# Second normalisation moved from the gate phase into the second attention pass

## The reference

```
x = x + conv1x1(gn(x), weight[unique(labels)]) + bias           # L0
x = x + linear_attention(gn(x))                                 # L1: qkv and a 5x5 depthwise + pointwise copy of it, 32 heads of 16, projection, batch norm
x = x + spatial_gate(gn(x))                                     # L2
x = x + softmax_attention(gn(x))                                # L3: v = gn(x); out = gamma * o + v
gn(v) = (v - mean) / sqrt(var + 1e-5), over a group of 8 channels and 49 positions
```

## Time and profile before

| | |
|---|---|
| median of 3 runs | 2304.32 us (2300.87 to 2311.59) |
| the profiled execution | 2306.92 us, its span 2305.0 us |
| TensorE busy | 1888.4 us (82%) |
| VectorE busy | 1408.7 us (61%) |
| ScalarE busy | 898.2 us (39%) |
| GpSimd busy | 274.6 us (12%) |
| moved by DMA | 279.45 MB |

### The profile page before, as it was taken

The page is one execution under the profiler, slowest core; times in us unless marked ns, Lnnn a source line. Parts: engine busy times, 40 slices in busy tenths (PEclk is TensorE's granted clock), DMA queues, the critical chain, the costliest instruction groups (busy, mean ns, idle before and its releaser), DMA issues. The chain is left out here.

```text
span 2305.0 us, 40585 instructions
## 1 busy us (share of the span) xinstructions
PE 1888.4 (82%) x15572; PEld 1215.3 (53%) x15572; DVE 1408.7 (61%) x2847; ACT 898.2 (39%) x2181; POOL 274.6 (12%) x77
## 2 busy tenths in 40 slices
PE   2799999999999999778778999994377776876768
PEld 1355555566666665566656677762134443444446
DVE  4676677765555554322222455554899989999984
ACT  0444444444444445333333444441123333233332
POOL 1000000000000000000000000001243434434340
PEclk9899999999999999899888999997578888887879
DMA  2122322375657656888878665642112112121101
GB/s 96 46 81 71 105 71 77 113 197 171 188 166 215 187 163 165 191 222 217 214 220 218 164 153 160 156 113 74 42 42 70 46 54 70 57 68 56 59 28 43
DMA packets 264469, 279.45 MB, mean 121 GB/s; under 512 B 208788, under 2 KB 234772, under 8 KB 264280
## 3 DMA queue, kind: packets, MB, share of 16 engines
q1 hardware_dynamic: 264120, 276.59, 42.8%
q0 software_dynamic: 160, 0.26, 0.0%
HBM read 161.21 MB, written 115.61 MB: 120 GB/s over the span
## 5 line engine op out<-in xcount | busy, mean ns | idle before, releaser
L484 DVE TENSOR_TENSOR vk<-p_vk,mask_vo 128x512 f32<-128x512 f32 x256 | 176.8, 691 | 556.7 <-PE p_vk L378 556.7
L1449 POOL TENSOR_TENSOR rstd<-var,minus_half 128x32 f32<-128x32 f32 x32 | 173.9, 5433 | 1896.3 <-DVE var L1025 1896.3
L414 PE MATMUL p_dw<-tw,qd 98*64 98x98 f32 x3072 | 244.0, 295 | 90.7 <-ACT agg_out L627 63.2
L414 PEld LDWEIGHTS p_dw<-tw,qd 98*64 98x64 f32 x3072 | 200.4, 206 | 154.7 <-ACT agg_out L627 80.7
L627 ACT ACTIVATE agg_out<-p_dw 128x294 f32<-128x294 f32 x256 | 106.4, 416 | 332.2 <-PE p_dw L414 254.0
L600 ACT ACTIVATE half_b<-p_qkv 98x384 f32<-98x384 f32 x256 | 125.2, 489 | 233.6 <-PE p_qkv L337 231.7
L437 PE MATMUL p_g<-o,w_proj 128*128 128x392 f32 x512 | 206.5, 529 | 3.0 <-DVE var L540 2.4
L337 PE MATMUL p_qkv<-w_qkv,half_a 128*98 128x384 f32 x512 | 190.8, 496 | 6.7 <-DVE half_a L556 6.7
L337 PE MATMUL p_qkv<-w_qkv,z_odd 128*98 128x384 f32 x512 | 190.4, 495 | 1.8 <-DVE z_odd L556 1.8
L390 PE MATMUL p_out<-vk,qr 128*49 128x136 f32 x2048 | 173.6, 291 | 1.0 <-DVE oN L499 1.0
L635 ACT ACTIVATE o<-p_turn 128x196 f32<-128x196 f32 x256 | 85.2, 333 | 163.0 <-PE p_turn L399 162.1
(11 more groups left out here) (176 smaller groups left out, 3191.4 us busy)
## 6 DMA issues: line engine op xcount, KB each, us to landing
qkv_scratch<-half_b SPq DMA_DIRECT2D x32, 1176.0 KB
qd<-qkv_scratch SPq DMA_DIRECT2D x64, 588.0 KB
agg_scratch<-agg_out SPq DMA_DIRECT2D x128, 294.0 KB, 5.5
tw<-in_w_toep SPq DMA_DIRECT2D x128, 220.5 KB
x_scratch<-xb SPq DMA_DIRECT2D x32, 784.0 KB, 5.2
half_a<-agg_scratch SPq DMA_DIRECT2D x48, 392.0 KB, 6.9
half_b<-agg_scratch SPq DMA_DIRECT2D x48, 392.0 KB, 6.7
half_a<-in_x SPq DMA_DIRECT2D x16, 784.0 KB, 4.8
```

The source lines that it names most:

```text
L414: mm = pe.matmul(p_dw[NP * cp:NP * cp + NP, PR * s:PR * s + PR], qd[:, QB % 2, :, ch - QB_CH * qb], tw[:, SB % 2, :, 6 * (F % SB_FILLS) + ...
L484: v.tensor_tensor(dst[:, :, 0:128].rearrange("p k (c n) -> p k c n", c=HC), src[:, :, 0:2 * D].unsqueeze(2).to_broadcast([128, 4, HC, 2 * D]),
L1449: done(g.tensor_tensor(rstd[k][:, :, :].rearrange("p t b -> p (t b)"), var[k][:, :], W["minus_half"][:, :], ALU.pow), f"rstd{k + 2}")
```

## The change

In layer_one_phase the second norm is made of xb as soon as the projection of a chunk of the second pass has been added. V_AT and PE_AT get slots for it two rounds later (ahead = -2): gate_sum, gate_centre, gate_square_sum, gate_var and gate_scale on VectorE, two gate_stat products on TensorE, a_gate_square and a_gate_root on ScalarE (the root as in the first pass: a square root, a reciprocal and one Newton step). The result lies in z_odd, which the first pass no longer needs, and SP stores it to a new scratch tensor z2_scratch. The mean per channel goes into a constant tile W["gap"]. The step range has 5 more steps at its end.

In gate_and_attention_phase everything of the second norm is gone. z2 has two buffers and is loaded from the scratch tensor one round ahead, when the chunk two before has been gated. The rounds are 20, with the chunks ahead r, gate r-1, norm3 r-2, attend r-3, leave r-4. The rest of the order is as before. The load of x2 for the gate's sum stays.

```diff
-        FIRST, LAST = -UN - 3, GT + UN + 1
+        FIRST, LAST = -UN - 3, GT + UN + 6
...
-                 (3, "a"): [("l0", 3, 1)], (4, "b"): [("stat", 2, 1)], (4, "c"): [("proj", 0, -1)],
+                 (3, "a"): [("l0", 3, 1)], (1, "a"): [("gate_stat", 0, -2)], (3, "c"): [("gate_stat", 1, -2)],
+                 (4, "b"): [("stat", 2, 1)], (4, "c"): [("proj", 0, -1)],
...
-        V_AT = {(0, "a"): [("proj", 3, -2)], (0, "b"): [("var", 0, 1)], (1, "a"): [("scale", 0, 1)],
+        V_AT = {(0, "a"): [("proj", 3, -2)], (0, "b"): [("var", 0, 1)], (0, "c"): [("gate_sum", 0, -2)],
+                (1, "b"): [("gate_centre", 0, -2)], (3, "b"): [("gate_square_sum", 0, -2)], (4, "a"): [("gate_var", 0, -2)],
+                (5, "a"): [("gate_scale", 0, -2)], (1, "a"): [("scale", 0, 1)],
...
+            elif what == "gate_stat":
+                pe.wait_ge(gate_summed, 2 * (n - chunks) + k + 1)
+                mm = pe.matmul(bank[:, 0:KT * NB], W["mask8"][:, :], stat[:, k, :], start=True, stop=True)
...
+        def v_gate(v, what, n):
+
+            c2, gate = n - chunks, tiles(z_odd[:, :])
+            if what == "gate_sum":
+                v.wait_ge(pg_read, turn["proj", n, 3] + 1)
+                v.tensor_reduce(stat[:, 0, :], by_image(xb[:, n % 2, :, :]), AX.X, ALU.add).then_inc(gate_summed, 1)
+            elif what == "gate_centre":
+                v.wait_ge(pg_mm, turn["gate_stat", n, 0] + 1)
+                v.tensor_scalar(mean[:, :, :].rearrange("p t b -> p (t b)"), group(("gate_stat", n, 0))[:, 0:KT * NB],
+                                1.0 / (GS * S), None, ALU.mult).then_inc(pg_read, 1)
+                v.wait_ge(pg_read, turn["gate_stat", n, 0] + 1)
+                if c2 == 0:
+                    v.wait_ge(qkv_mm, 2 * GA)
+                else:
+                    v.wait_ge(z2_st, 16 * c2)
+                v.tensor_tensor(by_image(gate), by_image(xb[:, n % 2, :, :]), over_positions(mean[:, :, :]),
+                                ALU.subtract).then_inc(gate_centred, 1)
+                v.scalar_tensor_tensor(W["gap"][:, c2, :], stat[:, 0, :], 1.0 / S,
+                                       mean[:, :, :].rearrange("p t b -> p (t b)"), ALU.mult, ALU.subtract).then_inc(gap_raw, 1)
+            elif what == "gate_square_sum":
+                v.wait_ge(gate_squared, c2 + 1)
+                v.tensor_reduce(stat[:, 1, :], by_image(sq[:, :, :]), AX.X, ALU.add).then_inc(gate_summed, 1)
+            elif what == "gate_var":
+                v.wait_ge(pg_mm, turn["gate_stat", n, 1] + 1)
+                v.tensor_scalar(var[:, :], group(("gate_stat", n, 1))[:, 0:KT * NB], 1.0 / (GS * S), 1e-5,
+                                ALU.mult, ALU.add).then_inc(pg_read, 1)
+            else:
+                flat = rstd[:, :, :].rearrange("p t b -> p (t b)")
+                v.wait_ge(gate_std, c2 + 1)
+                v.reciprocal(root[:, :], std[:, :]).then_inc(gate_guess, 1)
...
+                v.tensor_tensor(W["gap"][:, c2, :], W["gap"][:, c2, :], flat, ALU.mult).then_inc(gap_ok, 1)
+                v.wait_ge(gate_squared, c2 + 1)
+                v.tensor_tensor(by_image(gate), by_image(gate), over_positions(rstd[:, :, :]),
+                                ALU.mult).then_inc(gate_scaled, 1)
...
+        def a_gate_square(a, c2):
+            a.wait_ge(gate_centred, c2 + 1)
+            wait(a, gate_summed, 2 * c2)
+            a.activation(sq[:, :, :], tiles(z_odd[:, :]), ACT.Square).then_inc(gate_squared, 1)
...
+            if u == 2 and chunks <= c - 2 < NP2:
+                a_gate_square(a, c - 2 - chunks)
+            if u == 4 and chunks <= c - 2 < NP2:
+                a_gate_root(a, c - 2)
...
         def sp_load_part(sp, P):
             sp.wait_ge(xb_st[P % 2], 16 * (P // 2))
+            wait(sp, gate_centred, P - 2 - chunks + 1)
...
+        def sp_store_gate(sp, c2):
+            sp.wait_ge(gate_scaled, c2 + 1)
+            sp.dma_start(z2_out[c2], tiles(z_odd[:, :])).then_inc(z2_st, 16)
...
-            if u == 2 and chunks <= c < NP2:
+            if u == 3 and chunks <= c < NP2:
                 sp_load_part(sp, c)
+            if u == 6 and chunks <= c - 2 < NP2:
+                sp_store_gate(sp, c - 2 - chunks)
...
-        def v_body(v, intake, norm2, gate, norm3, attend, leave):
+        def v_body(v, ahead, gate, norm3, attend, leave):
...
-            run(v_mean, norm2, 0)
-            run(v_centre, norm3, 1)
+            run(v_centre, norm3)
             run(v_picked, gate)
-            run(v_centre, norm2, 0)
...
             run(v_spread_of_sim, gate)
-            run(v_square_sum, norm2, 0)
             run(v_context, gate)
-            run(v_var, norm2, 0)
             run(v_probs, attend)
-            run(v_sum, intake, 0)
             run(v_x3, gate)
-            run(v_scale, norm2, 0)
-            run(v_gap, norm2)
-            run(v_scale, norm3, 1)
+            run(v_scale, norm3)
             run(v_x4, attend, 0)
...
         def pe_sums(pe, it):
-            wait(pe, "z2", it + 1)
+            pe.wait_ge(z2_ok[it % 2], 16 * (it // 2 + 1))
...
         def g_gapped(g, it):
 
-            wait(g, "gapm", it + 1)
+            g.wait_ge(z2_ok[it % 2], 16 * (it // 2 + 1))
             wait(g, "gap_mm", it)
...
-        def sp_load(sp, it):
-
-            wait(sp, "centred2", it)
+        def sp_load_normed(sp, it):
+
+            wait(sp, "gated", 2 * it - 2)
             settle(sp, sems["met_sp"])
-            sp.dma_start(x2_in[:, :, :], x2[it]).then_inc(sems["x_in"], 16)
+            sp.dma_start(z2[it % 2][:, :, :], z2_in[it]).then_inc(z2_ok[it % 2], 16)
...
             run(sp_load_gate, gate)
-            run(sp_load, intake)
+            if ahead == 0:
+                sp_load_normed(sp, 0)
+            if ahead is not None and ahead + 1 < chunks:
+                sp_load_normed(sp, ahead + 1)
             run(sp_store, leave)
...
-                    body(eng, *[r - k if 0 <= r - k < chunks else None for k in range(6)])
+                    body(eng, *[r - k if 0 <= r - k < chunks else None for k in range(5)])
 
-            peeled(0, chunks + 5)
+            peeled(0, chunks + 4)
```

More of the change, by code:

```diff
@@ L319, in due @@
                 n = g // UN + ahead
-                if 0 <= n < (NP2 if what == "proj" else chunks):
+                if what == "proj":
+                    here = 0 <= n < NP2
+                elif what.startswith("gate"):
+                    here = chunks <= n < NP2
+                else:
+                    here = 0 <= n < chunks
+                if here:
                     yield what, n, k
@@ L576, in v_slot @@
         def v_slot(v, g, slot):
             for what, n, k in due(V_AT, g, slot):
-                v_group(v, what, n, k)
+                if what.startswith("gate"):
+                    v_gate(v, what, n)
+                else:
+                    v_group(v, what, n, k)
         def v_step(v, g):
@@ L1017, in v_square_sum, with v_sum @@
[L1017 to L1037 removed]
+        def v_sum(v, it):
+            wait(v, "x3", it + 1)
+            wait(v, "g_mm3", 2 * it)
+            done(v.tensor_reduce(stat[:, :], by_image(x3[it % 3][:, :, :]), AX.X, ALU.add), "sum3")
@@ new lines, in v_mean, with v_centre @@
+        def v_mean(v, it):
+            wait(v, "g_mm3", 2 * it + 1)
+            wait(v, "centred3", it)
+            done(v.tensor_scalar(mean[:, :, :].rearrange("p t b -> p (t b)"), p_wide[:, 1, 0:KT * NB],
+                                 1.0 / (GS * S), None, ALU.mult), "mean3")
+        def v_centre(v, it):
+            wait(v, "mean3", it + 1)
+            wait(v, "z3", it)
+            done(v.tensor_tensor(by_image(zc[:, :, :]), by_image(x3[it % 3][:, :, :]),
+                                 over_positions(mean[:, :, :]), ALU.subtract), "centred3")
@@ new lines, in v_square_sum, with v_var, v_scale @@
+        def v_square_sum(v, it):
+            wait(v, "squared3", it + 1)
+            done(v.tensor_reduce(stat[:, :], by_image(sq[:, :, :]), AX.X, ALU.add), "sum3")
+        def v_var(v, it):
+            wait(v, "g_mm3", 2 * it + 2)
+            done(v.tensor_scalar(var[:, :], p_wide[:, 1, 0:KT * NB], 1.0 / (GS * S), 1e-5,
+                                 ALU.mult, ALU.add), "var3")
+        def v_scale(v, it):
+            wait(v, "rstd3", it + 1)
+            wait(v, "o_mm", 4 * it - 4)
+            done(v.tensor_tensor(by_image(z3[it % 2][:, :, :]), by_image(zc[:, :, :]),
+                                 over_positions(rstd[:, :, :]), ALU.mult), "z3")
@@ L1326, in pe_out, with pe_body @@
                 done(mm, "o_mm")
-        def pe_body(pe, intake, norm2, gate, norm3, attend, leave):
+        def pe_body(pe, ahead, gate, norm3, attend, leave):
             def run(step, chunk, *more):
@@ L1418, in a_beta, with a_body @@
                                   ACT.Copy), "bt_ev")
-        def a_body(a, intake, norm2, gate, norm3, attend, leave):
+        def a_body(a, ahead, gate, norm3, attend, leave):
             def run(step, chunk, *more):
```

(4 more changed lines are left out.)

178 lines of the change are left out of this document (68 added, 110 removed).

## The result

The changed kernel takes 2369.9 us (median of 4 runs, 2366.2 to 2376.9) against 2306.5 us of the kernel before in the same series (2300.9 to 2311.6): a ratio of 1.0279, 95% interval 1.0244 to 1.0314. It is slower by 63 us. The forecast was 2336 us, the range 2290 to 2365; the direction was right and the size was half of the truth.

A forecast was written before the change was run, and what follows sets the result against it. It took a TensorE-ScalarE ring without slack to bound the second pass's later rounds, DMA its first, VectorE the gate phase; +42 +16 +20 -15.9 -8.8 -21.2 = +32 gave 2336 us, range 2290 to 2365.

The forecast's parts named there:

- rivals 1, 2 and 4: Pass absorbs the work: 2293, chance 0.20; busy time counts in gate phase: 2262, 0.05; agg comes late: 2356, 0.10.
- The ten TensorE-bound rounds: Second pass, P=20 to 29: added work in order delays TensorE 4.2 us a round, 42 us for ten.
- The four waits: TensorE-bound rounds: gate_stat behind gate_sum, p_out behind late oN, turn behind ScalarE's square, second gate_stat behind sum of squares.
- Tail: Last chunks of the second pass: P=30 adds 7.7 us, P=31's uncovered chain 12.3; together 20, between 14 and 22.
- The four DMA-bound rounds, +16: Second pass, P=16 to 19: new 784 KB store costs 3.9 us each at 206 GB/s; ends 0 and 32 us.
- Start of the gate phase: z2 comes by DMA where x2 did, so the first picked starts at about 1601 instead of 1616.85: gain 15.9 us.
- First two rounds: Gate phase, 1616.85 to 1689.11: centring, scale and gap go from both, intake's sum and a wait from the first: gain 8.8.
- Steady rounds, -21.2: Gate phase, 13 rounds: VectorE sheds 7.3 us each but most is cover; rounds become 39.6 us, gain 21.2.
- none of which changes: Gate phase start: group sums, hot, gapped on GpSimd and the gap product, between z and first picked, stay the same.
- The wait of x4 for its store, worth 0: Gate phase: store behind the z2 load lands 0.2 us late; the 1.59 us wait for p_wide takes it up.
- rival 3: Gate phase: three DMAs in flight land x4's store 3 us later, 1.6 counting in 11 rounds: +18, 2354; chance 0.15.
- From the round at 2224.61 on nothing is different: Last 80 us of the gate phase: those rounds have no second norm before either, so 0 us.

The follow-up runs named there:

- re-spaced: Changed kernel with the second pass's normalisation work moved to other slots and its square made by GpSimd instead of ScalarE: 2328.0 us, ratio 1.0084.
- the doubled run: Changed kernel with the second pass re-spaced, plus the first four chunks' z stored twice: 2335.7 us, ratio 1.0114.
- gapped in the hole: Changed kernel with GpSimd's gapped also waiting for the round's scaling z3, so it runs while VectorE is idle ahead of x4's addition: 2332.1 us, ratio 1.0100.
- the changed one with the store first: Changed kernel with the store of x4 queued ahead of the z2 load on SP in the gate phase: 2373.2 us, ratio 1.0282.
- both repairs: Changed kernel with the re-spaced second pass (square on GpSimd) and gapped made after the round's scaling: 2292.9 us, ratio 0.9942.

## Why the prediction was right and wrong

- *The direction, and the small chances of rivals 1, 2 and 4:* right. The pass did not absorb the work in the order that it was given, and busy time did not count in the gate phase. No wait of TensorE for agg appeared in its TensorE-bound rounds.
- *The ten TensorE-bound rounds, 4.2 us each, 42 in all:* right in every mechanism, small in size: 4.7 each, 47.2. The four waits summed to what was laid out (31.6 us for a round against 31.5 forecast). What failed is the step from one round to ten: it took all rounds at full clock, and four of them ran at 0.95 and took 32.8. The work added on VectorE was sized at 9 us a round and measured 8.2 (22.83 less 14.64); re-spaced, 7.8 us of it cost 0.3.
- *Tail:* P=31's chain came to 11.8 us for 12.3, that of P=30 to 10.5 for 7.7. (The listed terms of the first add up to 12.0, or 12.2 with var itself.)
- *The four DMA-bound rounds, +16:* wrong. The step that failed is pricing 784 KB at the 206 GB/s of the earlier trace rows, as though that rate were the most that the engines move. It rose to 221 with the store added, and to 266 in one stretch of the doubled run; the kernel before moved 237 in its next round already (1179.90 to 1238.40, at a share of 0.91). The lower end, 0, was the answer: the four rounds take 243.0 us for 245.8. The store of P=20 moves by 7 us between two executions that are alike up to there (1292.1 and 1299.0), so a price of a few us would not show, but 16 would. The price of one more store after that, some 2 us, is only suggested.
- *Start of the gate phase:* 16.4 us for 15.9. *First two rounds:* 4.1 for 8.8. The held-up addition takes 2.6 in each of them, but that is not the whole of it: with gapped in the hole the second is back at 0.16, and the two rounds gave only 1.0 more (5.1). The rest of this miss stays open.
- *Steady rounds, -21.2:* wrong by 33.2 us, the main miss. The failed step is "none of which changes" and what goes with it: gapped was priced as work of GpSimd, an engine with time to spare, and never laid against what VectorE does at its new place. It lost its wait for VectorE's gapm, which had kept it at the end of the round, and slid to the first moment at which GpSimd is free, right behind sstd. With only that undone the rounds gave 21.3. The prediction also sets VectorE's 7.3 us against groups that add up to 7.5 (1.8, 3.7 and 2.0), which changes nothing.
- *The wait of x4 for its store, worth 0, and rival 3:* right against appearances. The trace shows 46 us of waits for it, and taking them away gave nothing; the prediction's own sign of being wrong, x4 waiting for a DMA, misled. The 1.59 us wait for p_wide took up the lateness as reckoned; the rival would have begun at 1.6, and its landing 3 us later than 6.9 did not come: in the rounds of that wait the store landed after 6.8 to 7.5 us. With gapped in the hole, where x4 shows the same wait, the store was not moved.
- *"From the round at 2224.61 on nothing is different":* right for the work, 4.5 us off in the time. These two stretches, of the changed kernel and of the kernel with gapped in the hole, hold the same instructions:

```profile
2283.53:2368.40 84.87, 66.05 (x321) 47.04 (x319) 42.19 (x61) 24.16 (x56) 12.45 (x3) 0.84 0.07 29
```

```profile
2249.12:2329.50 80.38, 61.30 (x321) 42.57 (x319) 42.19 (x61) 24.14 (x56) 12.45 (x3) 0.89 0.08 31
```

In the profiles of all kernels that have these instructions, these last 80 us take 80.4 us (9 of 13, among them the kernel before and the changed one with the store first) or 84.8 to 84.9 (4 of 13, among them the changed kernel and both repairs), the longer ones at a granted clock of 0.82 or 0.84, the shorter ones at 0.87 or 0.89. So this is no effect of the change. What decides between the two, no run shows.

## What to carry to other kernels

Moving an instruction on an idle engine is not free: lay its new place against what the neighbouring engine does there, and above all look where it slides to when the wait that held it back is taken away. In a pass whose bound engine has no slack, cost moved work by the order it is put in, not by idle shares: the same 8 us of VectorE came with 4.7 us a round in one order and 0.3 in another (0.6 of the difference is ScalarE's square, which went to GpSimd). A long wait in a profile is worth only what the next wait behind it does not take up, so try the slack before repairing the wait.

## What was new of the hardware

A GpSimd product of 128x1568 on SBUF and certain VectorE instructions exclude each other for their whole length. Held: the addition on 64x8 with one fp32 operand in SBUF (0.16 to 2.77 us), the same with two (2.77), the centring with two operands in SBUF of 128x1568 (1.79 to 4.02). Not held: the reciprocal of den from SBUF to SBUF (0.25 us beside the square) and products that read PSUM and one tile in SBUF (vk, 0.69 us).

It works the other way round as well, and it is not every GpSimd instruction. Both show in one round of the kernel before, GpSimd first, then VectorE:

```profile
1867.48 5.43 POOL L1449 TENSOR_TENSOR rstd<-var,minus_half 128x32 f32<-128x32 f32 x1 [19.28 <-DVE var L1025]
...
1884.97 4.30 POOL L1456 TENSOR_TENSOR gapped<-z,gapm 128x1568 f32<-128x1568 f32 x1 [3.71 <-DVE gapm L1050]
```

```profile
1869.51 0.56 DVE L1113 TENSOR_TENSOR sim<-sim,gap_sim 64x392 f32<-64x392 f32 x1
...
1870.69 0.16 DVE L1115 TENSOR_SCALAR smean<-ssum 64x8 f32<-64x8 f32 x1
...
1884.81 1.78 DVE L1036 TENSOR_TENSOR z<-zc,rstd 128x1568 f32<-128x1568 f32 x1
```

gapped was issued 0.16 us behind VectorE's scaling of z and took 4.30 us, against 2.81 to 2.82 where it starts first. But GpSimd's power for rstd (128x32), though it lasts 5.43 us, held neither a VectorE product with two operands in SBUF (0.56 us) nor an instruction from SBUF to SBUF on 64x8 of the same kind as the held addition (0.16 us). So the length of a GpSimd instruction alone does not say what it costs. Whether its operation or the size of its operands decides, no run here shows.

The Trainium skill ("SBUF — State Buffer", SBUF: two separate sides) states it so: the port pair that VectorE and GpSimd share is an exclusive lock, taken for a whole instruction by whichever starts first, by VectorE if it runs in a mode with two ports or has two inputs in SBUF. With the GpSimd products the runs agree, with 2.23 us added to the centring and 2.6 to the addition; that the addition ran in a mode with two ports is what the rule needs for it, and no run here shows it. With the GpSimd power they do not agree: the product with two inputs in SBUF ran beside it at its own 0.56 us, and there the measurement decides. It is the rule that spoke against this change, and the prediction did not weigh it.

The clock granted to TensorE can be lower in rounds with added waits: of the ten rounds with four waits of about 1 us, six have 1.00 and four 0.95, while the rounds of the re-spaced pass, with 27.5 to 27.6 us every time, have 1.00, and so have those with one wait of 1.09 or 1.34 us put back. What decides between the two in a given round, no run here shows.
